# Attention and a 4-bit feed-forward: reordering three engines' queues where plain steps pass to block products

## The reference

```python
x = x + _L0_xattn_ref(_layernorm(x), ctx_1024, Wq, Wk, Wv, Wo, gq, gk)
x = x + _L0_ffn_ref(_layernorm(x), gate codes and scales, up ..., down ...)

# _L0_ffn_ref, with xt of (1600, 512) and MLP_DIM = 4096
Wg, Wu, Wd = dequant_nvfp4(gate...), dequant_nvfp4(up...), dequant_nvfp4(down...)
gate = jnp.einsum('th,nh->tn', xt, Wg)
up = jnp.einsum('th,nh->tn', xt, Wu)
gelu = jnp.tanh(0.7978845608028654 * (gate + 0.044715 * gate ** 3)) * gate * 0.5 + gate * 0.5
inter = gelu * up
out = jnp.einsum('tn,hn->th', inter, Wd)
```

## Time and profile before

| | us |
|---|---|
| median of 3 runs | 1980.84 |
| lowest, highest | 1976.94, 1981.91 |
| the profiled execution | 1979.3 |
| its span in the trace | 1977.5 |
| TensorE busy | 1950.2 |
| VectorE busy | 1603.4 |
| GpSimd busy | 1140.7 |
| ScalarE busy | 1007.4 |

### The profile page before, as it was taken

How to read it: one execution, slowest core, us unless ns; L and a number is a source line. 1 busy time by engine, 2 the same in 40 slices (tenths; PEclk the granted TensorE clock), 3 DMA queues, 4 the chain that set the end, 5 groups by cost and what they waited for, 6 DMA issues and landing times.

```text
span 1977.5 us, 33604 instructions
## 1 busy us (share of the span) xinstructions
PE 1950.2 (99%) x11232; PEld 1860.2 (94%) x11232; DVE 1603.4 (81%) x2994; ACT 1007.4 (51%) x2338; POOL 1140.7 (58%) x1273
## 2 busy tenths in 40 slices
PE   8999999999999999999999999989999999999999
PEld 7899899999999999999999999989999999999998
DVE  7877887788877787877787887888888888888875
ACT  5565565555555555555555553344444444444442
POOL 6756665523435332444333335798888888887871
PEclk9999999999999999999999999999999999999999
DMA  6435434332332323333323324211111110111101
GB/s 205 139 97 177 153 122 135 127 109 89 125 117 92 129 92 111 112 119 103 108 90 109 124 77 131 66 33 33 40 36 33 33 33 33 33 33 33 33 1 67
DMA packets 93514, 174.54 MB, mean 88 GB/s; under 512 B 13264, under 2 KB 49760, under 8 KB 91296
## 3 DMA queue, kind: packets, MB, share of 16 engines
q1 hardware_dynamic: 93344, 172.39, 26.7%
HBM read 139.00 MB, written 33.36 MB: 87 GB/s over the span
## 4 chain that ended last, share of the span: by engine, by line
PE 89%; DVE 6%; issue 1%; ACT 1%; POOL 1%; DMA 0%; SPq 0%; DVEq 0%; ACTq 0%; POOLq 0%
PE psum L425 44%; PE psum L801 20%; PE psum L456 6%; PE psum L489 4%; PE psum L497 4%; PE psum L512 3%; PE psum L518 3%; PE psum L513 3%; PE psum L575 1%; DVE ysum L1482 1%; PE psum L528 1%; DVE tT_lo L1219 1%; DVE g L1449 0%; DVE g L1444 0%; ACT g L1025 0%
## 5 line engine op out<-in xcount | busy, mean ns | idle before, releaser
L909 ACT ACTIVATE work<-psum,stats,q_rstd 100x361 f32<-100x361 f32 x256 | 163.6, 650 | 169.3 <-DVE stats L1320 169.2
L1219 DVE TENSOR_TENSOR kaT_lo<-psum,kaT_hi 128x488 fp32r<-128x488 f32 (+2 forms) x384 | 213.8, 612 | 38.9 <-ACT kaT_hi L849 38.9
L425 PE MATMUL psum<-wk,ctxT_hi 128*122 128x512 f32 x768 | 240.9, 395 | 0.0
L1909 POOL TENSOR_TENSOR inter_lo<-g,inter_hi 128x400 fp32r<-128x400 f32 x128 | 143.5, 1126 | 125.6 <-ACT inter_hi L849 124.7
L849 ACT CAST kaT_hi<-psum 128x488 fp32r<-128x488 f32 (+2 forms) x384 | 178.8, 540 | 51.4 <-PE psum L497 50.7
L1753 POOL TENSOR_TENSOR k_ss<-k_ss,power 122x4 f32<-122x4 f32 x192 | 193.8, 1009 | 16.0
L1751 POOL TENSOR_SCALAR k_ss<-k_ss 122x4 f32<-122x4 f32 x192 | 37.0, 193 | 269.6 <-DVE k_ss L1275 269.6
L1310 DVE TENSOR_REDUCE stats<-psum 100x2 f32<-100x722 f32 x128 | 115.7, 904 | 80.1 <-PE psum L456 80.1
L425 PE MATMUL psum<-inter_hi,down_hi 128*128 128x400 f32 x512 | 176.7, 345 | 3.6 <-POOL inter_lo L1909 2.4
L425 PE MATMUL psum<-inter_lo,down_hi 128*128 128x400 f32 x512 | 176.2, 344 | 0.0
L425 PE MATMUL psum<-inter_hi,down_lo 128*128 128x400 f32 x512 | 175.9, 344 | 0.0
(11 more groups left out here) (267 smaller groups left out, 6156.2 us busy)
## 6 DMA issues: line engine op xcount, KB each, us to landing
head_w<-spill_sq SPq DMA_DIRECT2D x48, 512.0 KB, 3.5
head_w<-spill_so SPq DMA_DIRECT2D x46, 512.0 KB, 3.8
wk<-spill_sk SPq DMA_DIRECT2D x12, 1024.0 KB, 4.8
wv<-spill_sv SPq DMA_DIRECT2D x48, 256.0 KB, 2.8
spill_so<-head_w SPq DMA_DIRECT2D x16, 512.0 KB, 3.0
spill_sq<-head_w SPq DMA_DIRECT2D x14, 512.0 KB, 3.0
wk_raw<-in_ctxT SPq DMA_DIRECT2D x12, 361.0 KB, 3.9
spill_sk<-wk SPq DMA_DIRECT2D x4, 1024.0 KB, 6.2
```

The source lines that it names most:

```text
L425: last = e.matmul(out, a_, b_, start=begins and i == 0, stop=ends and i == len(passes) - 1)
L909: e.activation(attn[h][:, 0:SKV], bank[3 + h][0:SQ, 0:SKV], ACT.Exp, bias=st[:, h:h + 1], scale=rq[:, i * QH + h:i * QH + h + 1], accum_ou ...
L1219: e.tensor_tensor(dst, src, high.bitcast(F32), ALU.subtract).then_inc(S[sem], 1)
L1909: e.tensor_tensor(il[:, :], gact[n % 3][:, :], ih[:, :].bitcast(F32), ALU.subtract).then_inc(S["il"], 1)
```

## The change

It touches three queues from tile 10 to the end of pair 1; TensorE's and SyncE's queues stay word for word as they were, and all instructions are the same ones.

- Passage, VectorE: argument(14) before down_add(20), and active(14), active(15) before the token casts of h = 1; token_lo(1, 1, *) moves into pair 0.
- Passage, ScalarE: square(14) before inter_hi(13); the first four block_hi before square(15); token_hi(1, 0, *) behind tangent(15); token_hi(1, 1, *) into pair 0 behind the first two evictions.
- Passage, GpSimd: weight_sums(2, 1) and inter_lo(13) before rebuild(1); token_sums(1) behind the first six block_lo instead of before inter_lo(13).
- Pair 0, VectorE: of four coming_codes only the first (spread of the gate codes) stands before combine(0, 0, 1); its joined comes after combine(0, 0, 2); the up codes move into pair 1, before combine(1, 0, 0).
- Pairs 0 and 1, GpSimd: coming_weights(3, 0) before inter_lo(17) as before, coming_weights(3, 1) only after inter_lo(19); down_lo(2, *) before them.
- Pair 1: down_hi(3, *) on ScalarE and decode_scaled, down_lo(3, *) on GpSimd move from the middle to the pair's end, behind all block casts.

The core of the diff:

```diff
@@ scalar_program, passage
+            for n in (10, 11):
+                square(n)
+                tangent(n)
+                inter_hi(n)
+            square(12)
+            tangent(12)
+            for j in range(4):
+                token_hi(0, 1, j)
+            inter_hi(12)
+            square(13)
+            tangent(13)
+            square(14)
+            inter_hi(13)
+            tangent(14)
+            for i in range(2):
+                for k in range(2):
+                    block_hi(2, k, i)
+            square(15)
+            inter_hi(14)
+            tangent(15)
+            for j in range(4):
+                token_hi(1, 0, j)
+            inter_hi(15)
@@ scalar_program, pairs
                 evict(p, 1, 0)
                 if p > 0:
                     inter_hi(n - 1)
+                else:
+                    for j in range(4):
+                        token_hi(1, 1, j)
...
-                if h == 1 and jt + 1 < JT:
+                if h == 1 and 1 < p < PAIRS - 1:
                     down_hi(jt + 1, 0)
                 evict(p, 1, 2)
-                if h == 1 and jt + 1 < JT:
+                if p == 0:
+                    down_hi(2, 0)
+                    down_hi(2, 1)
...
                     for k in range(2):
                         block_hi(jt + 1, k, 6)
+                if p == 1:
+                    down_hi(3, 0)
+                    down_hi(3, 1)
@@ vector_program, pairs
+                if p == 1:
+                    coming_codes(0, 2)
+                    coming_codes(0, 3)
                 combine(p, 0, 0)
                 combine(p, 1, 0)
...
+                if p == 0:
+                    token_lo(1, 1, 0)
+                    token_lo(1, 1, 1)
+                    down_add(q + 4)
+                    token_lo(1, 1, 2)
+                    token_lo(1, 1, 3)
+                    argument(n)
+                    down_add(q + 5)
+                    gelu(n)
+                    gated(n)
+                    down_add(q + 6)
+                    coming_codes(0, 0)
+                    combine(0, 0, 1)
+                    down_add(q + 7)
...
                 combine(p, 0, 2)
                 if 0 < p < PAIRS - 1:
                     down_add(q + 6)
+                if p == 0:
+                    coming_codes(0, 1)
@@ gpsimd_program, passage
             inter_lo(12)
+            weight_sums(2, 1)
+            inter_lo(13)
             rebuild(1)
-            token_sums(1)
-            inter_lo(13)
-            weight_sums(2, 1)
...
@@ gpsimd_program, pairs
+                if p == 1:
+                    coming_weights(3, 1)
                 inter_lo(n)
-                if h == 0 and jt + 1 < JT:
+                if p == 0:
+                    down_lo(2, 0)
+                    down_lo(2, 1)
+                    coming_weights(3, 0)
...
+                if p == 1:
+                    decode_scaled(3 * PIECES + 4)
+                    decode_scaled(3 * PIECES + 5)
+                    down_lo(3, 0)
+                    down_lo(3, 1)
```

111 lines of the change are left out of this document (51 added, 60 removed).

## The result

Over 20 runs each, the kernel before takes 1979.95 us in the median (1976.25 to 1981.91) and the changed one 1982.22 (1980.89 to 1984.22): a ratio of 1.0013, with a 95% interval of 1.0007 to 1.0019. That is 1.4 to 3.8 us slower, real but within the 0.3% that was called no change. The forecast was 1981.1, and no change. The profiled execution of the changed kernel took 1984.22 us, with a span of 1982.4.

The account below looks back on a forecast made before the run. TensorE, busy 1950.2 of 1977.5 us, bounds the kernel. New losses of 13.8 us against 13.6 removed give about 0.2 to 0.3 slower: 1981.1 from the median 1980.84, no change (0.73), range 1975.5 to 1986.5.

Parts of the forecast that it names:

- The passage: From 1280.78 to 1341.97, 265 matmuls take 61.2 us instead of 48.0; these 13.2 us are all it can give.
- A: Down(24) starts 2.60 us late on inter_lo(13), slow starts take 1.64 more; all 4.2 us were to go.
- Pair 0: New stalls at product(0,0,3) on the low block, 0.5 us, and product(0,0,4) on the eviction, 1.2; together 1.7, bounds 0 and 3.5.
- Pair 1: New losses: 1.2 us on gelu(18), 2.5 at down(32) on GpSimd's inter_lo behind joined(3,0), 1.6 of half clock.
- Pair 2: Product(2,0,2) waits for the moved down step, starting 9.6 us after pair 2's start T (8.9 to 10.4), plus 1.6 half clock.
- short block: Rival 1: the block at pair 2 is short and the gain stands; 1974.4 if GpSimd's bound were reached, chance 0.14.
- the tail: From pair 2's start to product(2,0,2): 9.6 us instead of 4.35, a loss of 5.2, bounds 8.9 to 10.4.
- C: In pair 0, product(0,0,6) waits 3.5 us for combine(0,0,1) behind four coming_codes, slow starts follow; 5.2 us in all.
- Rival 1: The block at pair 2 is short and the gain stands, decode_scaled(23) done by about T + 3; 1974.4, chance 0.14.
- Rival 2: VectorE reaches joined(3,0) late, up to 5.5 us, 1986.6; slower than 0.3% from 5.6 us; chance 0.13.
- Rival 3: The clock stays up after the new waits, both prices of 1.6 us fall: 1977.9; inside no change, 0.73.
- Rival 4: No stall at down(32): pair 2 starts at 1331.7, end 1976 to 1979; mostly inside no change, 0.73.

Follow-up runs that it names:

- e5: Kernel before, with only inter_lo(13) on GpSimd moved between rebuild(1) and token_sums(1): ratio to before 1.0006, +0.22 us by the marks.
- e3: Changed kernel with the four gate block sums weight_sums(3,0) behind inter_lo(19) instead of before inter_lo(17): ratio to before 1.0004, 1.59 us less than the changed kernel.
- e2: Changed kernel with the down step of the fourth weights moved on from pair 1's end into pair 2: ratio to before 0.9993, 3.98 us less than the changed kernel.
- e6: Kernel before, with only the down step of pair 1 moved from the middle to the pair's end: ratio to before 1.0013, +1.31 us.
- e9: Changed kernel with block casts 3 and 4 and their block_lo back ahead of tangent(21) and inter_lo(21): ratio to before 0.9989, 3.85 us less than the changed kernel.
- e1: Changed kernel with the down step of pair 1 put back in the middle: ratio to before 0.9994, 2.86 us less than the changed kernel.
- e8: e4 with three VectorE places changed (argument(16) earlier, joined(3,0) behind argument(18), down_add(33) before the down-code spread): ratio to before 0.9989, 3.20 us worse than e4.
- e7: Changed kernel with all four coming_codes of pair 0 back before combine(0,0,1) on VectorE: ratio to before 1.0026, +2.11 us against the changed kernel.
- e4: Changed kernel with the edits of e2 and e3 together: ratio to before 0.9973, 6.05 us less than the changed kernel.
- e10: e4 with the fourth down codes' spread behind argument(21) and joined between gelu(22) and argument(23) on VectorE: ratio to before 0.9983, 1.27 us worse than e4.

## Why the forecast held, step by step

**The passage.** Right. A is gone with its slow starts, pair 0 starts 13.10 after gate_up(7), forecast 13.08. GpSimd in the changed kernel answers to the earlier trace rows:

```profile
1280.24 1.05 POOL L1947 TENSOR_TENSOR inter_lo<-g,inter_hi 128x400 fp32r<-128x400 f32 x1 [0.79 <-ACT inter_hi L849]
1281.25 2.07 POOL L1921 TENSOR_TENSOR raw<-xT_hi,xT_lo 128x400 f32<-128x400 f32 x2
...
1312.76 2.52 POOL L1875 TENSOR_TENSOR gate_stage<-value,gate_scale 128x512 f32<-128x512 f16 x2 [2.67 <-DVE value L1448]
...
1319.12 3.64 POOL L1947 TENSOR_TENSOR inter_lo<-g,inter_hi 128x400 fp32r<-128x400 f32 x3
```

Inter_lo(13) stands ahead of rebuild(1) and is done 3.1 us before down(24) starts at 1284.39. e5 shows that its place was the cause of the wait; the change also had to put token_sums(1) off for the gain to last.

**Pair 0.** Right in kind: 0.52 on the low block (0.5 forecast) and 1.00 on the eviction (1.2). Pair 1 starts at +35.05, forecast +34.4. From start to start the two waits are 0.69 and 1.16 beyond the usual 0.18, 0.15 more than the 1.7 of the forecast. A small third wait at 1309.49 is 0.23. And the second start after each of the three comes 0.26 to 0.29 later instead of 0.18, about 0.3 in all: a wait costs a little more than its bracket says. These make up the missing 0.67.

**Pair 1.** The chain was right, its terms short: 30.32 us instead of 29.2, which is most of what the forecast missed. The rows at 1312.76 and 1319.12 show it: GpSimd waits 2.67 us for joined(3,0), then decodes, sums and the inter_lo. VectorE in the changed kernel, the combine that releases product(0,0,6), and joined:

```profile
1306.27 0.56 DVE L1486 TENSOR_TENSOR gate_kept<-psum,gate_kept 128x400 f32<-128x400 f32 x1
...
1307.44 1.51 DVE L1460 SCALAR_TENSOR_TENSOR g<-g,gate_kept 128x400 f32<-128x400 f32 x1
...
1311.99 0.69 DVE L1448 TENSOR_TENSOR value<-value,gate_packed 128x512 int32<-128x512 int32 x1
```

Joined is done at 1312.68, 1.0 later than forecast on the scale of gate_up(7): argument(17), the row at 1307.44, took 1.51 and gelu(17) behind it 0.97, where the forecast had 4.0 us for some eight such rows. Counted from start to start, with the late second start, down(32) costs 3.25 instead of 2.5 and the wait for gelu(18) 1.62 instead of 1.2; the slow starts cost 1.56 (1.6 forecast). That is the 1.1 us. e3 shows that the wait at down(32) has that cause: with the sums behind the inter_lo it is gone.

**Pair 2.** Right, at the short end: product(2,0,2) starts at T + 8.99, forecast 9.6 with bounds 8.9 to 10.4, and the wait of 4.46 lies just under the 4.5 to 6 that were to show it. The eight block_lo take 5.91 us (5.6 to 7.0 forecast), with starts 0.68 to 0.71 apart except one of 1.02. VectorE is busy beside the first five, with rows that read PSUM and then the first row below, which reads two tiles of SBUF; the long block_lo, at 1342.90, is the one that starts while that row runs. So the short rows are not only those with a quiet VectorE, as the forecast had it. Then VectorE is idle for 6.24 us:

```profile
1342.46 0.90 DVE L1477 SCALAR_TENSOR_TENSOR g<-g,up_kept 128x400 f32<-128x400 f32 x1
1349.60 0.57 DVE L1465 SCALAR_TENSOR_TENSOR g<-g,psum 128x400 f32<-128x400 f32 x1 [6.24 <-ACT g L1025]
```

The outcome lies 0.6 us under the forecast's 9.6 and 0.1 over the T + 8.9 at the short rows, which is what the Trainium skill, GPSIMD Engine Reference, section Specifications, with its SBUF interfaces shared with VectorE, would have given; the trace agrees here, though no run varied VectorE's work alone. e2 (wait gone), e6 and e9 (wait halved) show the cause. What the forecast did not say is that the casts' place carries half of the term: it named block_hi(3,0,3) behind tangent(22) as a link, but priced the rival "short block" only by GpSimd's total work. The 1.6 us of half clock behind the wait came as forecast: from product(2,0,2) to pair 3 it is 21.2 us, against 19.55 before.

**The sum.** +0.67 in pair 0, +1.1 in pair 1, -0.6 in the tail: 1.2 later than the forecast's 0.2 to 0.3 slower, and that is the measured +1.48. The call of "no change" rests on two large sums, 13.6 and 13.8, that nearly cancel, and their terms were each met within about 1 us; that the errors had different signs is luck. So is part of the nearness of 1981.1 to 1982.22: the three runs that the forecast started from have a median of 1980.84, the twenty 1979.95, and the difference was forecast as +0.25 us and measured as +2.3 by the medians.

**Slips in the forecast.** The range is given as the bounds and 1 us, but 1980.84 with -4.9 and +3.8 and that 1 us is 1974.9 to 1985.6, not 1975.5 to 1986.5; the result lies in either. The "eleven" slow starts after A and C are ten and nine by the spacings of 0.33 us, with one of 0.47 ahead of C's nine; the price of 1.6 is read rightly. And the row at 1290.93, on gated(15), is three products ahead of the one at 1294.95, not four.

**The rivals.** Rival 1 (the gain stands) did not come: it needed the second decode by about T + 3, and that ends at T + 7.5. In e9, with four block_lo fewer in the chain, it ends at T + 5.2, which gives 3.85 us; so a fair part of the gain hung on one more move, though not the 5.9 us of the rival. Rival 2 (joined late) came with 1.0 of the 5.6 us at which it decides. Rival 3 (clock stays up) fell: both waits were followed by slow starts. Rival 4 (no stall at down(32)) fell, and e3 tells what it would have given: 1.59 us less than the changed kernel, about level with before, and not the 1976 to 1979 that it was priced at.

## What to carry to other kernels

Ask of each removed wait which engine gets the time and what is queued there: 8.15 us won at pair 1 were all given back by two chains that ended on engines whose work was merely put off. When a step is moved behind a block of other work, count the block from the moment its first instruction can start; moving half of the block into a gap of idle time just ahead of it can be worth as much as moving the step (3.85 us in e9, 2.86 in e1, 3.98 in e2). And before an instruction is moved ahead of another, look whether it would have waited anyway: the one behind it may have been filling that wait for nothing (e8).

## What the runs showed of the hardware

**The clock does not go by the length of one wait alone.** After waits of 3.00 and 4.46 us in the changed kernel nine starts are 0.33 us apart, at a granted clock of 0.50, which is 1.2 of 2.4 GHz. After waits of 2.12 and 2.15 us (e6 and e9, product(2,0,2)) none are, and after 2.43 in the earlier trace rows ten are. The number does not grow with the wait: after 7.04 us (e7) it is seven, after 5.32 (e3) eleven, and after the same wait at down(32), 3.00 and 3.03 us, nine in the changed kernel and fifteen in e1. In e8 the wait ahead of nine slow starts is 1.50 us, with smaller ones of 0.37 and 0.26 before it, while in e4 1.69 us and in e10 1.70 us cost no clock. The small waits near it set e8 apart, but that is an argument and not a test. The Trainium skill, TensorE: Matmul & The Clock Gate, section What's actually happening, says the clock goes by how busy the array has been recently; the traces agree in direction, since in the stretches read here each wait of 2.43 us or more is followed by slow starts at once or a few matmuls later, and of the shorter ones outside such stretches only e8's is. What exactly it takes stays open here; no run varied only that.

**VectorE and GpSimd hold each other up over SBUF, and which row started first decides.** The changed kernel's trace has 204 block_lo of one size (128x256). Of these, 106 start while a VectorE row is running that reads SBUF alone, and all 106 last 0.91 us or more (median 1.07, up to 1.63). Of the 98 others, which start beside a VectorE row that reads PSUM, or beside none, 91 last 0.73 to 0.76 and seven 1.29 to 1.30. On VectorE the same shows in the rows of argument, gelu and gated. The 112 that read two SBUF tiles (g with gate_kept or up_kept) last 0.70 us or more in all 101 cases where they start while a GpSimd row is running, and 0.57 or 0.58 in the 11 others; those that read g and a PSUM bank last 0.56 to 0.57, whatever GpSimd does. The row of 1.51 us at 1307.44 that made joined late is one of the 101. These are counts over one trace, not an experiment on it; the trace of the kernel before gives 109 of 109, and 104 of 104 against none of 8. So a chain on GpSimd is best summed with the rows of a stretch in which VectorE reads what it will read there; whether VectorE is busy does not tell.
